# A Mamba-2 mixer and an FFN on one core: the running sums of dA sent as rows through DRAM and back to all partitions, and the exponents formed by VectorE in two operations a tile

## The reference

```python
dt = softplus(dt + dt_bias)
A = -jnp.exp(A_log)
...
A_cumsum = jnp.cumsum(A, axis=-1)
L = jnp.exp(segsum(A))
Y_diag = jnp.einsum('bclhn,bcshn,bhcls,bcshp->bclhp', C, B, L, x)
...
Y_off = jnp.einsum('bclhn,bchpn,bhcl->bclhp', C, states, state_decay_out)
```

## Time and profile before

| | |
|---|---|
| median of 3 runs | 955.85 us (955.42 to 956.91) |
| the profiled execution's own time | 955.01 us |
| its span | 953.3 us |
| mean granted TensorE clock | 0.971 of full speed |

### The profile page before, as it was taken

How to read it: one execution, slowest core, us unless ns; L and a number is a source line. 1 busy time by engine, 2 the same in 40 slices (tenths; PEclk the granted TensorE clock), 3 DMA queues, 4 the chain that set the end, 5 groups by cost and what they waited for, 6 DMA issues and landing times.

```text
span 953.3 us, 16507 instructions
## 1 busy us (share of the span) xinstructions
PE 892.7 (94%) x5632; PEld 773.0 (81%) x5632; DVE 704.9 (74%) x1566; ACT 532.2 (56%) x1016; POOL 72.3 (8%) x104
## 2 busy tenths in 40 slices
PE   4777789899999999999999999999999999999997
PEld 3446678788898888888888888888888888888887
DVE  6767988787769776786779876786779776867453
ACT  4743486448645775448735674547635674456232
POOL 2101000200011000200020000200020000200000
PEclk9787899999999999999999999999999999999999
DMA  4111100010002000010001000010002000100010
GB/s 135 33 58 49 32 18 12 23 45 1 1 23 67 0 0 22 22 44 0 0 22 66 0 0 22 31 35 0 0 22 67 1 1 13 45 12 1 1 35 12
DMA packets 18651, 23.13 MB, mean 24 GB/s; under 512 B 1584, under 2 KB 15152, under 8 KB 18608
## 3 DMA queue, kind: packets, MB, share of 16 engines
q1 hardware_dynamic: 18176, 22.56, 7.4%
q10 hardware_dynamic: 432, 0.03, 0.0%
HBM read 14.19 MB, written 4.19 MB: 19 GB/s over the span
## 4 chain that ended last, share of the span: by engine, by line
PE 78%; DVE 10%; issue 6%; POOL 3%; ACT 2%; DMA 1%; POOLq 0%; DVEq 0%; SPq 0%; ACTq 0%
PE gate_bank L493 6%; PE up_bank L493 6%; PE up_bank L495 6%; PE up_bank L494 6%; PE gate_bank L495 5%; PE gate_bank L494 5%; PE down L493 5%; PE down L495 5%; PE mixer L493 5%; PE down L494 5%; PE mixer L495 5%; PE mixer L494 5%; PE mixer L573 3%; DVE xbc L904 2%; PE mixer L552 2%
## 5 line engine op out<-in xcount | busy, mean ns | idle before, releaser
L493 PE MATMUL down<-wd_hi,in_hi 128*128 128x256 f32 x512 | 145.1, 283 | 0.7 <-DVE in_lo L1035 0.7
L495 PE MATMUL down<-wd_hi,in_lo 128*128 128x256 f32 x512 | 144.0, 281 | 0.0
L494 PE MATMUL down<-wd_lo,in_hi 128*128 128x256 f32 x512 | 143.8, 281 | 0.0
L904 DVE SCALAR_TENSOR_TENSOR xbc<-mixer,chan,xbc 128x510 f32<-128x510 f32 (+1 forms) x162 | 110.9, 685 | 27.8 <-ACT xbc L703 26.1
L760 ACT ACTIVATE in_hi<-act_sb 128x512 fp32r<-128x512 f32 (+1 forms) x144 | 83.4, 579 | 65.3 <-PE down L495 53.7
L1049 DVE SCALAR_TENSOR_TENSOR act_sb<-up_bank,act_sb 128x512 f32<-128x512 f32 (+1 forms) x144 | 90.4, 628 | 37.5 <-PE up_bank L495 18.5
L774 ACT ACTIVATE act_sb<-gate_bank 128x512 f32<-128x512 f32 (+1 forms) x144 | 79.0, 548 | 67.7 <-PE gate_bank L495 67.0
L493 PE MATMUL gate_bank<-hT_hi,wg_hi 128*128 128x512 f32 (+1 forms) x288 | 111.4, 387 | 3.1 <-DVE wg_lo L1102 3.1
L493 PE MATMUL up_bank<-hT_hi,wu_hi 128*128 128x512 f32 (+1 forms) x288 | 108.4, 376 | 6.4 <-DVE act_sb L1049 6.4
L495 PE MATMUL up_bank<-hT_hi,wu_lo 128*128 128x512 f32 (+1 forms) x288 | 107.8, 374 | 0.0
L494 PE MATMUL up_bank<-hT_lo,wu_hi 128*128 128x512 f32 (+1 forms) x288 | 107.8, 374 | 0.0
(11 more groups left out here) (200 smaller groups left out, 1936.2 us busy)
## 6 DMA issues: line engine op xcount, KB each, us to landing
xbc<-in_u_t_dram SPq DMA_DIRECT2D x7, 512.0 KB, 3.6
h_sb<-in_u_dram SPq DMA_DIRECT2D x7, 512.0 KB, 3.8
h_res<-h_sb SPq DMA_DIRECT2D x7, 512.0 KB, 2.9
out_dram<-h_res SPq DMA_DIRECT2D x7, 512.0 KB, 2.9
scales<-in_ffn_s_dram SPq DMA_DIRECT2D x24, 128.0 KB, 2.1
packed<-in_ffn_w_dram SPq DMA_DIRECT2D x8, 96.0 KB, 2.1
xbc<-in_u_t_dram SPq DMA_DIRECT2D x2, 256.0 KB, 2.8
xbc<-in_W_in_dram SPq DMA_DIRECT2D x1, 512.0 KB, 6.2
```

Source lines behind the costliest of these rows:

```text
L493: nc.tensor.matmul(dst, lh, rh, start=first, stop=False, skip_group_check=True)
L494: nc.tensor.matmul(dst, lh, rl, start=False, stop=False, skip_group_check=True)
L495: return nc.tensor.matmul(dst, ll, rh, start=False, stop=last, skip_group_check=True)
L904: ins = stt(acc[:, :, d:], src[:, :, 0:SEQ - d], chan[:, c:c + 1], acc[:, :, d:], ALU.mult, ALU.add)
```

## The change

The running sums are made once for a group, by step A: with dA in three copies of [128, 4 tiles, 8 heads] (a part rounded to a fixed grid, the part that it leaves, negated, and dA whole), one matmul gives all running sums as rows, [96, 128], and a second gives them by token. ScalarE takes exp of 32 of the rows and of one part by token, VectorE copies the other rows and two small operands, and SP writes the 96 rows to a DRAM tensor `spread`, waits for that, and reads them back with each row on all partitions: for each tile `low` and `dec` of [128, 8 x 128], 512 KB each, and for each odd tile `state_decay`, 256 KB in two DMAs. Step L on VectorE forms the exponents in `dec` in two operations of 1024 elements (subtract the tile's own sum by token, then take the minimum with 0 and subtract `low`), step X on ScalarE takes exp in place, step W is what VectorE did after D, with the same three instructions. R, D and E are gone. `dec`, `low` and `cb` now have two buffers; CB1 and CB0 are made in slot 2, and the small chain that makes dt (`dt_chain`) starts earlier and has one link more (`LINKS`).

```diff
 USES = {
-    "full": ["dt", "x4", "x5", "x0", "z0", "x1", "z1", "x2", "z2", "x3", "z3", "CB0", "XT0",
-             "D0a", "D0b", "Y0", "XT1", "D1a", "D1b", "E0", "Y1", "Yoff0", "CB1", "XT2", "D2a", "D2b", "S0",
-             "op0", "Y2", "XT3", "S1", "D3a", "D3b", "E1", "op1", "Y3", "Yoff1", "S2", "op2", "S3", "op3"],
...
+    "full": ["dt", "x4", "x5", "x0", "z0", "x1", "CB0", "CB1", "z1", "x2", "z2", "A", "x3", "z3", "XT0", "Y0", "XT1",
+             "Y1", "Yoff0", "XT2", "S0", "op0", "Y2", "XT3", "S1", "op1", "Y3", "Yoff1", "S2", "op2", "S3", "op3"],
...
 SLOTS = {
-    "full": [["x5"], ["x0", "z0"], ["x1", "z1"], ["x2", "z2"], ["x3", "z3"], ["CB0", "R0", "XT0"],
-             ["D0"], ["R1", "Y0", "XT1"], ["D1"], ["R2", "Y1", "CB1", "g0", "XT2"], ["D2", "S0"],
-             ["R3", "op0", "g1", "Y2", "XT3"], ["S1", "D3"], ["op1", "g2", "Y3"], ["S2", "op2", "g3"],
-             ["S3", "op3", "ln1"], ["ln2"]],
...
+    "full": [["x5"], ["x0", "z0"], ["x1", "CB0", "CB1", "z1"], ["x2", "z2"], ["A", "x3", "z3"], [],
+             ["L0", "XT0", "X0", "W0"], ["Y0"], ["L1", "XT1", "X1", "W1"], ["Y1", "g0"],
+             ["L2", "XT2", "X2", "S0", "W2"], ["op0", "g1", "Y2"], ["L3", "XT3", "X3", "S1", "W3"],
+             ["op1", "g2", "Y3"], ["S2", "op2", "g3"], ["S3", "op3", "ln1"], ["ln2"]],
...
+             ("x0", 1): [9], ("x0", 2): [10], ("x0", 3): [11], ("z0", 0): [12], ("x1", 1): [13], ("x1", 2): [14],
+             ("x1", 3): [15], ("z1", 0): [16], ("x2", 1): [17], ("x2", 2): [18], ("x2", 3): [19], ("z2", 0): [20, 21]},
...
-        dt_sb, dA = sb("dt_sb", [P, NT, H]), sb("dA", [P, NT, H])
...
+        dA = sb("dA", [P, 3, NT, H])
+        sum_hi, low_exp = sb("sum_hi", [P, NT * H]), sb("low_exp", [P, NT, H])
+        dec, low = sb("dec", [P, 2, H, P]), sb("low", [P, 2, H, P])
+        state_decay = sb("state_decay", [P, DI])
+        cb = sb("cb", [P, 2, 3, P])
...
+            def spread_sums(g, which=range(NT)):
+                if 0 in which:
+                    wait_for((a_act, g, 1), (a_rows, g, 1))
+                    sp.dma_start(spread, rows).then_inc(rows_out.sem, 16)
+                    wait_for((rows_out, g, 1))
+                for i in [i for i in which if i < tiles(g)]:
+
+                    if i >= 2:
+                        wait_for((exp_in, g, i - 1))
+                    elif kind_of(g) == "first" and i:
+
+                        sp.wait_ge(winz_ok.sem, JT)
+                    sp.dma_start(low[:, i % 2, :, :], of_tile(1, i).partition_broadcast(P)).then_inc(lo_in[i % 2].sem, 16)
+                    if i >= 2:
+                        wait_for(ready_at(g, f"Y{i - 2}"))
+                    elif kind_of(g) != "first":
+                        wait_for(ready_at(g - 1, f"Y{tiles(g - 1) - 2 + i}"))
+                    sp.dma_start(dec[:, i % 2, :, :], of_tile(0, i).partition_broadcast(P)).then_inc(hi_in[i % 2].sem, 16)
+                    if i % 2:
+                        if i > 1:
+                            wait_for((y_step, g, 3))
+
+                        for a in range(2):
+                            by_head = of_tile(2, i).rearrange("(j a) l -> a j l", a=2)[a]
+                            sp.dma_start(by_block(state_decay[a * HP:(a + 1) * HP, :]), by_head.partition_broadcast(HP))\
+                                .then_inc(e_in.sem, 16)
...
-                elif kind == "D":
...
-                        upper, lower = R_of(g)
-                        nc.tensor.matmul(bank(g, use)[:, :], after_r[:, :], upper[:, hs, :], start=True, stop=False)
-                        nc.tensor.matmul(bank(g, use)[:, :], after_r[:, :], lower[:, hs, :], start=False,
-                                         stop=True).then_inc(ready(g, use)[0].sem, 1)
-                    if i % 2:
...
+                elif name == "A":
+
+                    wait_bank(pe, name, g)
+                    wait(pe, dA_ok, g, 2)
+                    b = bank(g, name)
+                    nc.tensor.matmul(b[0:3 * NT * H, 0:P], dA[:, :, :, :].rearrange("p a t h -> p (a t h)"), tri[:, :],
+                                     start=True, stop=True)
+                    nc.tensor.matmul(b[:, P:P + 2 * NT * H], tri[:, :], dA[:, 0:2, :, :].rearrange("p a t h -> p (a t h)"),
+                                     start=True, stop=True).then_inc(ready(g, name)[0].sem, 1)
...
-                elif kind == "R":
-                    wait_R(act, i, g)
-                    for h in range(H):
-                        ins = nc.scalar.activation(R_of(g)[0][:, h, :], tri[:, :], ACT.Copy,
-                                                   scale=f32(dA_hi[:, i, h:h + 1]))
...
-                    for n, use in enumerate((f"D{i}a", f"D{i}b")):
-                        wait_ready(act, use, g)
-                        nc.scalar.activation(dec_of(g, i)[:, 4 * n:4 * n + 4, :],
-                                             bank(g, use)[:, :].rearrange("p (h l) -> p h l", h=4),
...
+                    if i < tiles(g - 1) // 2:
+                        wait_ready(act, f"Yoff{i}", g - 1)
+                    nc.scalar.activation(cb[:, i, 1, :], bank(g, f"CB{i}")[:, P:2 * P], ACT.Copy).then_inc(cb_act.sem, 1)
+                elif name == "A":
+                    wait_ready(act, name, g)
+                    n = NT * H
+                    nc.scalar.activation(rows[2 * n:3 * n, :], bank(g, name)[2 * n:3 * n, 0:P], ACT.Exp)
+                    nc.scalar.activation(low_exp[:, :, :].rearrange("p t h -> p (t h)"), bank(g, name)[:, P + n:P + 2 * n],
+                                         ACT.Exp).then_inc(a_act.sem, 1)
+                elif kind == "X":
+                    wait(act, exp_in, g, i + 1)
+                    d = dec[:, i % 2, :, :]
+                    nc.scalar.activation(d, d, ACT.Exp).then_inc(dec_ok.sem, 1)
...
+
+                    wait_ready(dve, "A", g - 1)
+                    ins = tt(dA[:, 2, 0:n, :], dt_sb[:, 0:n, :], a_neg[:, :].unsqueeze(1).to_broadcast([P, n, H]),
                              ALU.mult)
                 elif k == 19:
-                    ins = nc.vector.tensor_copy(dA_hi[:, 0:n, :], dA[:, 0:n, :])
+                    ins = ts(cut, dA[:, 2, 0:n, :], CUT, None, ALU.add)
+                elif k == 20:
+                    ins = ts(dA[:, 0, 0:n, :], cut, CUT, None, ALU.subtract)
                 else:
-                    ins = tt(dA_lo[:, 0:n, :], dA[:, 0:n, :], f32(dA_hi[:, 0:n, :]), ALU.subtract)
-                ins.then_inc(dA_ok.sem if k == 20 else dt_step.sem, 1)
+                    ins = stt(dA[:, 1, 0:n, :], cut, CUT, dA[:, 2, 0:n, :], ALU.subtract, ALU.subtract)
...
-                elif kind == "R":
-                    wait_R(dve, i, g)
-                    tt(R_of(g)[1], tri[:, :].unsqueeze(1).to_broadcast([P, H, P]),
-                       f32(dA_lo[:, i, :]).unsqueeze(2).to_broadcast([P, H, P]), ALU.mult).then_inc(R_l.sem, 1)
+                    tt(cb[:, i, 0, :], bank(g, f"CB{i}")[:, 0:P], tri[:, :], ALU.mult)
...
+                elif name == "A":
+
+                    wait(dve, a_act, g, 1)
+                    n = NT * H
+                    nc.vector.tensor_copy(rows[0:2 * n, :], bank(g, name)[0:2 * n, 0:P]).then_inc(a_rows.sem, 1)
+                    nc.vector.tensor_copy(sum_hi[:, :], bank(g, name)[:, P:P + n])
+
+                    tt(dt_low[:, 0:tiles(g), :], dt_sb[:, 0:tiles(g), :], low_exp[:, 0:tiles(g), :], ALU.mult)\
+                        .then_inc(a_ok.sem, 1)
+                elif kind == "L":
+                    wait(dve, a_ok, g, 1)
+                    wait(dve, hi_in[i % 2], g, i // 2 + 1)
+                    d = dec[:, i % 2, :, :]
+
+                    tt(d, d, sum_hi[:, i * H:(i + 1) * H].unsqueeze(2).to_broadcast([P, H, P]), ALU.subtract)\
+                        .then_inc(fall_ok.sem, 1)
+                    wait(dve, fall_ok, g, i + 1)
+                    wait(dve, lo_in[i % 2], g, i // 2 + 1)
+                    stt(d, d, 0.0, low[:, i % 2, :, :], ALU.min, ALU.subtract).then_inc(exp_in.sem, 1)
                 elif kind == "XT":
                     use = f"XT{i}"
                     wait_ready(dve, use, g)
...
-                elif kind == "D":
...
+                elif kind == "W":
+                    d = dec[:, i % 2, :, :]
+                    wait(dve, dec_ok, g, i + 1)
                     if i % 2 == 0:
                         nc.vector.tensor_copy(tail[:, :], d[:, :, P - 1]).then_inc(tail_ok.sem, 1)
-                        if kind_of(g) != "first":
-                            x_tail(i, g)
+                        x_tail(i, g)
                         wait(dve, tail_ok, g, i // 2 + 1)
                     wait(dve, cb_ok, g, i // 2 + 1)
-                    tt(d[:, :, :], d[:, :, :], cb[:, 2 * (i % 2):2 * (i % 2) + 1, :].to_broadcast([P, H, P]),
+                    tt(d, d, cb[:, i // 2, 2 * (i % 2):2 * (i % 2) + 1, :].to_broadcast([P, H, P]),
                        ALU.mult).then_inc(W_ok.sem, 1)
```

156 lines of the change are left out of this document (57 added, 99 removed), and 19 rows, old and new, of tables (LINKS, SLOTS, USES).

## The result

The changed kernel takes 963.95 us (962.66 to 966.15, four runs) against 955.94 for the kernel before: a ratio of 1.0088, with a 95% interval of 1.0068 to 1.0108. It is 8 us slower, where 945.2 was forecast. Further on, two executions that fell far outside the rest, one of e8 (1213.83 us) and one of the kernel before beside e9 to e11 (1738.07), are left out of medians and ratios.

The account below looks back on a forecast made before the run. TensorE's instructions were taken to bound groups 1 to 6: -5.1 plus 3.5 of waits, -1.6 each, -9.6 for six. With LAST -1.0 and the start 0, -10.6 from 955.0 gives 944.4, plus 0.8: 945.2 us (own range 938 to 952; overall 929 to 966).

Parts of the forecast that it names:

- What TensorE loses and gains: Full group: six four-matmul steps of 0.92 out (5.5 us), step A in (0.4), net -5.1 us.
- The four waits: New TensorE waits in a full group, at CB0, unit 5's gate, Y0 and Y2: 3.5 us in sum.
- The gate of unit 5: Full group: the gate product waits 1.3 us for gelu(4), behind A and a GELU table load of 1.28.
- Y0: Full group, slot 7: TensorE waits 0.7 us for VectorE's product, behind L0 and the exp.
- Y2: Full group, slot 11: TensorE waits 1.1 us for tile 2's product, as VectorE leaves slot 9 late.
- CB0: Full group, slot 2: TensorE waits 0.4 us for the pair of SiLU products.
- The transfers: Full group: write and broadcasts of tile 0 taken as hidden behind units 4 and 5, 1 to 4 us to spare.
- LAST, FIRST, group 0: Outside the full groups: LAST -1.0 us; FIRST and group 0 between -3 and +3 together, taken as 0.
- B: Rival, chance 0.15: tile 0's broadcasts land 2.2 us after L0 asks and the clock falls; 969 us.
- A: Rival, chance 0.28: the four waits are smaller; 923 us if all fall away, 934 if half stay.
- D: Rival, chance 0.10: VectorE is later in slots 6, 9 and 10, its three waits twice as long; 960 us.
- C: Rival, chance 0.05: a ScalarE table switch costs twice its row in the chain to gelu(4); 954.3 us.

Follow-up runs that it names:

- e8: e6 with step z3 of full groups also moved from slot 4 into empty slot 5: 940.96 us, 0.9858 of the kernel before.
- e9: e6 with the first of L's two operations left out in FIRST and group 0: 944.32 us, 0.9880 of the kernel before.
- e11: e6 with tanh in place of exp in FIRST and group 0: 950.89 us, 0.9956 of the kernel before.
- e5: Changed kernel with the two exps of step A replaced by copies: 955.08 us, 0.9987 of the kernel before.
- e7: Changed kernel with step z3 of full groups moved from slot 4 into empty slot 5: 955.54 us, 0.9992 of the kernel before.
- e4: Changed kernel with group 0's write two weight loads earlier and FIRST's tile 1 broadcasts one load later: 954.46 us, 0.9998 of the kernel before.
- e6: e4 with ScalarE taking weight 22 after the exp of tile 1 in group 0: 949.80 us, 0.9944 of the kernel before.
- e10: e6 with both of L's operations cut to one on a single element in FIRST and group 0: 937.72 us, 0.9833 of the kernel before.

## Why the prediction was wrong

**What bounds the kernel** was right for groups 1 to 6 and LAST, and the reading that VectorE bounds group 0 was right too; only its price was not drawn.

**What TensorE loses and gains** was right. A takes 0.36 from its start to that of x3 (0.4 taken). A full group lost 2.3 with 3.0 of waits, so what was taken out is 5.3 net (5.1 worked out).

**The four waits.** The gate of unit 5: 1.3 worked out, 1.33 measured, and shown by e5 to be the table load in the chain to gelu(4); e7 takes the wait away without taking the load away. The rows of the changed kernel, ScalarE's and then TensorE's:

```profile
344.36 1.28 ACT L789 ACT_TABLE_LOAD   x1
345.65 0.60 ACT L789 ACTIVATE act_sb<-gate_bank 128x512 f32<-128x512 f32 x1
```

```profile
346.30 0.50 PE L535 MATMUL gate_bank<-hT_hi,wg_hi 128*128 128x512 f32 x1 [1.33 <-ACT act_sb L789]
```

Y0: 0.7, measured 0.5. Y2: 1.1, measured 1.1 (its sum, 1.6 and 5.9 against 6.3, gives 1.2). CB0: 0.4, and the profile names no wait there; that term was mis-sized, since the pair of SiLU products ends at 323.48 and CB0 starts at 323.54, with x1 done at about the same time. So the group gained 2.3 and not 1.6.

**The transfers** were right in the full group: L0 was to ask 12.4 after the start of slot 4 and stands at 349.97, 12.55 after A's 337.42, with no DMA in its wait; `dec` of tile 0 landed 3 us before it, 6.0 after its issue at 341.00. But the step was worked out for the full group alone. It names SyncE and then counts from the moment the rows are ready, with nothing ahead in SyncE's queue. In group 0 and FIRST weight loads stand in that queue, each waiting for VectorE. Nothing in the prediction walks SyncE's order there, although the code calls `spread_sums` from among those loads.

**LAST, FIRST, group 0** is the step that failed, in its part on FIRST and group 0, as the prediction put it: "Between -3 and +3 together; I take 0, since each gives what the other takes". The runs put in its place +23.6: 10.5 from SyncE's order (e4 against the changed kernel: 4.7 in FIRST, 5.8 in group 0), about 2.6 from ScalarE's order behind weight 22 (e6), and 10.5 that stays. e10 shows L to be in that last part; that 7.3 of it are L less R is worked out and not measured, and the last 3 are open. These shares are from single profiles, and each holds what the granted clock gave back with the wait: FIRST's was 0.79 and then 0.85, group 0's 0.81 and then 0.84. The prediction had the 5.5 us for group 0, and set them against TensorE's 5 less. That was the error in reasoning: where VectorE bounds a stage, TensorE's time gives nothing back (in group 0 it was busy for 85.5 us after the change and 84.9 before). FIRST was not worked out at all.

LAST was forecast at -1.0 and came out at -1.9, but not by its terms. TensorE's new waits there are 1.2 ahead of CB0 (0.2 taken), 0.6 for gelu(4) and 0.6 ahead of Y0, 2.4 in all, as much as the instructions taken out. What LAST gained goes with the clock: 0.83 for 10 us of it in the kernel before (827.16 to 837.16), 1.00 in the same place after (837 to 847).

**The rivals.** B had a broadcast that is late for L0 and a clock that falls behind the wait, which group 0 shows (a DMA ends the wait ahead of L0, the prediction's own sign of B). It had the side and nearly the size of the result, 969, but by luck: it put the lateness down to the transfer's length and to the full groups, and there it didn't happen. dec0's 6.0 us were longer than the 5.3 that B took, but low0 and dec0 did not go one after the other: from low0's issue to dec0's landing it is 6.5 and not 10.6. It is luck too that 963.95 lies inside the range over all, 929 to 966: the upper part of that range stood for waits in the full groups. A and D didn't come: but for CB0's, the waits of the full group were those worked out. C didn't either: in the changed kernel the load ahead of gelu(4) starts at 344.36, takes 1.28, and the GELU starts at 345.65. The Trainium skill's page ScalarE: Activation LUTs, section "What ACT_TABLE_LOAD costs", gives a drain of about 1.38 us beside the load of 1.28. None is seen in these rows; the wait was 1.33 and not 2.7, and e5, which takes the load out, shortens a full group by 1.4.
